# First modulation of an adaLN block cut in two by feature, its gate row spread by 32-row groups

## What is computed

```python
x = L0_attn_data                                   # (2, 512, 512) f32
mod = (_silu(L0_c) @ L0_wmod).reshape(2, 6, 1, -1)  # c (2, 512), wmod (512, 3072)
sa, ca, ga, sb, cb, gb = (mod[:, 0], mod[:, 1], mod[:, 2], mod[:, 3], mod[:, 4], mod[:, 5])
ga = (2 * (ga >= 0) - 1) * jnp.maximum(jnp.abs(ga), 0.25)     # gb likewise
h = _layernorm(x) * (1 + ca) + sa
x = x + ga * (h @ (weight * block_mask).T + bias)   # 512x512, mask in 32x32 blocks
h = _layernorm(x) * (1 + cb) + sb
x = x + gb * ffn(h)      # silu(h w1') * (h w3') w2', each w with a rank-16 addition, HID 1376
```

## Time and profile before

| what | value |
|---|---|
| time, median of 3 runs | 253.67 us (253.4 to 253.71) |
| the profiled execution's own time | 253.31 us |
| its span, first to last instruction | 251.5 us |
| PE busy | 244.5 us (97%) |
| DVE, ACT, POOL busy | 134.3, 90.0, 96.8 us |
| granted TensorE clock | 0.996 of full |
| packets moved | 24.02 MB, mean 96 GB/s |

### The profile page before, as it was taken

The page is one execution under the profiler, slowest core; times in us unless marked ns, Lnnn a source line. Parts: engine busy times, 40 slices in busy tenths (PEclk is TensorE's granted clock), DMA queues, the critical chain, the costliest instruction groups (busy, mean ns, idle before and its releaser), DMA issues.

```text
span 251.5 us, 3398 instructions
## 1 busy us (share of the span) xinstructions
PE 244.5 (97%) x1202; PEld 193.4 (77%) x1202; DVE 134.3 (53%) x215; ACT 90.0 (36%) x152; POOL 96.8 (38%) x102
## 2 busy tenths in 40 slices
PE   7999999998999999999999999999999999999993
PEld 6757876886888888888888778888888888888772
DVE  3568599899899854654654631741233123312224
ACT  2358563843423465465432412122212221222110
POOL 1329792326423130330310360497356335633300
PEclk9999999999999999999999999999999999999998
DMA  6999990022324413313317630040000000000005
GB/s 187 385 367 408 414 384 21 3 86 83 83 83 126 128 42 122 85 46 116 92 46 106 44 19 0 12 154 0 3 1 0 0 0 3 0 0 0 3 1 168
DMA packets 12529, 24.02 MB, mean 96 GB/s; under 512 B 1240, under 2 KB 2648, under 8 KB 12512
## 3 DMA queue, kind: packets, MB, share of 16 engines
q1 hardware_dynamic: 12352, 23.65, 30.2%
q10 hardware_dynamic: 160, 0.15, 0.3%
HBM read 21.18 MB, written 2.10 MB: 93 GB/s over the span
## 4 chain that ended last, share of the span: by engine, by line
PE 88%; DMA 4%; DVE 2%; POOL 1%; SPq 1%; issue 1%; ACT 1%; DVEq 0%; POOLq 0%; ACTq 0%
PE up_b L1114 24%; PE up_a L1114 24%; PE acc L1128 8%; PE acc L1129 8%; PE acc L1127 8%; DMA wa<-in_weight 4%; PE acc L1064 4%; PE side L1095 2%; POOL ht_lo L399 1%; DVE xt L806 1%; PE side L1099 1%; PE side L1064 1%; PE acc L967 1%; PE up_a L991 1%; PE acc L1027 1%
## 5 line engine op out<-in xcount | busy, mean ns | idle before, releaser
L904 DVE TENSOR_TENSOR g<-up_b,g 128x512 f32<-128x512 f32 (+1 forms) x22 | 15.2, 690 | 64.5 <-PE up_b L1114 64.5
L1128 PE MATMUL acc<-w_lo,g_hi 128*128 128x512 f32 (+1 forms) x88 | 34.7, 394 | 0.0
L1129 PE MATMUL acc<-w_hi,g_lo 128*128 128x512 f32 (+1 forms) x88 | 34.7, 394 | 0.0
L1127 PE MATMUL acc<-w_hi,g_hi 128*128 128x512 f32 (+1 forms) x88 | 34.6, 394 | 0.0
L654 ACT ACTIVATE g<-up_a 128x512 f32<-128x512 f32 (+1 forms) x22 | 13.1, 597 | 58.8 <-PE up_a L1114 58.8
L794 DVE SCALAR_TENSOR_TENSOR raw<-side,raw 128x512 f32<-128x512 f32 (+2 forms) x33 | 21.5, 677 | 22.9 <-PE side L1095 16.3
L661 ACT ACTIVATE g_hi<-g 128x512 fp32r<-128x512 f32 (+1 forms) x22 | 13.9, 633 | 49.1 <-DVE g L904 49.1
L442 POOL TENSOR_TENSOR w_lo<-work,w_hi 128x512 fp32r<-128x512 f32 (+1 forms) x11 | 14.2, 1287 | 41.3 <-ACT w_hi L580 41.3
L573 ACT ACTIVATE w_hi<-raw 128x512 fp32r<-128x512 f32 (+2 forms) x33 | 20.3, 627 | 21.7 <-DVE raw L794 21.6
L908 DVE TENSOR_TENSOR g_lo<-g,g_hi 128x512 fp32r<-128x512 f32 (+1 forms) x22 | 22.7, 1033 | 8.7 <-ACT g_hi L661 8.4
L1114 PE MATMUL up_a<-ht_hi,w_lo 128*128 128x512 f32 (+1 forms) x88 | 24.2, 396 | 1.1 <-DVE w_lo L800 1.1
(11 more groups left out here) (161 smaller groups left out, 381.5 us busy)
## 6 DMA issues: line engine op xcount, KB each, us to landing
raw<-in_ffn SPq DMA_DIRECT2D x33, 256.0 KB, 2.7
wmod_sb<-in_wmod SPq DMA_DIRECT2D x4, 1024.0 KB, 11.5
xt<-in_x SPq DMA_DIRECT2D x8, 256.0 KB, 8.2
wmod_sb<-in_wmod SPq DMA_DIRECT2D x1, 2048.0 KB, 15.7
out<-xt SPq DMA_DIRECT2D x8, 256.0 KB, 2.5
mask_sb<-in_mask SPq DMA_DIRECT2D x4, 256.0 KB, 9.8
wa<-in_weight SPq DMA_DIRECT2D x4, 256.0 KB, 9.9
lora_raw<-in_lora SPq DMA_DIRECT2D x1, 512.0 KB, 10.4
```

Of the source, the lines that this page charges most:

```text
L904: nc.vector.tensor_tensor(g[0:w], up_b[0:w], g[0:w], ALU.mult).then_inc(g_ready, 1)
L1127: nc.tensor.matmul(acc[t][:], hi, down_hi[j][0:w], start=(j == 0), stop=False)
L1128: nc.tensor.matmul(acc[t][:], hi, down_lo[j][0:w], start=False, stop=False)
L1129: last = nc.tensor.matmul(acc[t][:], lo, down_hi[j][0:w], start=False, stop=(j == HT - 1))
```

## The change

SP: mask 0 is loaded ahead of the first modulation's weights. These weights are laid out anew on the host so that one 1 MB load holds shift and scale of features 0 to 255 (all rows of `wmod`), and a second, now behind masks and weights 0 and 1, those of features 256 to 511. The place of the second batch's `x`, ahead of the gate's weights, is the same in both kernels.

TensorE: each half of the first modulation has 16 matmuls of 128 columns, its own bank, copy, turn (one transpose) and `shift`/`one_plus`. Half 0 stands before the first `attend`; half 1 and the turn of chunk 3 behind `attend(0, 0, 0)`. Warm-up matmuls go from 26 to 28, fillers from five to two. The mask's block sums move, `gate_rows(0)` stands behind `attend(0, 2, 2)` instead of ahead of it, and the gate is spread by eight matmuls with 32-row operands, of which four (one for each group of rows) write four banks. The second modulation has 32 matmuls of 128 columns in place of 16 of 256.

ACT and DVE: `bias_high` and `bias_part` come first; ACT makes one more normed tile of pass 1 (DVE one less); the gate is copied by four instructions of 2 x 128 columns, one a bank; low-rank piece 1 comes later on both. POOL: the root of tiles 4 and 5 stands one step earlier, that of 6 and 7 behind the last `wa_lo`.

```diff
-WARM_MATMULS = 26
+WARM_MATMULS = 28
-GATE_COPIES = B
+GATE_COPIES = T
+CENTRED = {0: 2, 1: 2, 4: 4, 5: 4, 6: 6, 8: 8, 9: 8, 10: 10}
+NORMS_ACT = (2, 5, 8)
+NORMS_DVE = (2, 3, 4)
-FILL_TURN, FILL_H = 3, 2
+FILL_H = 2
...
+        def mods_done(q):
+            i, k = divmod(q, KT)
+            return 3 if PASSES[i][1] else 1 + k // 2
...
             load_x(0)
-            load_mod(SHIFT_A, GATE_A, wmod_a_loaded[0], slice(0, KT // 2))
             sp.dma_start(mask_sb[:, 0], mask[:, 0]).then_inc(mask_loaded[0], 16)
-            load_mod(SHIFT_A, GATE_A, wmod_a_loaded[1], slice(KT // 2, KT))
+            load_first_mod(0)
             sp.dma_start(wa[:, 0], weight[:, 0]).then_inc(wa_loaded[0], 16)
-            for k in range(1, KT):
-                load_attention(k)
+            load_attention(1)
+            load_first_mod(1)
+            load_attention(2)
+            load_attention(3)
             load_x(1)
...
             masked_weight_low(2)
             low(2)
+            root(T, 2)
             masked_weight_low(3)
-            root(T, 2)
             root(T + 2, 2)
             low(3)
...
+            def gate_copy(q):
+
+                act.wait_ge(spread_out, 1)
                 act.wait_ge(block_on_ready, KT)
-                nc.scalar.activation(gate_row_a[b], acc[2 + b][:], ACT.Copy).then_inc(gate_row_ready, 1)
+                src = acc[q][:, 2 * P:(2 + B) * P].rearrange("p (b n) -> p b n", b=B)
+                nc.scalar.activation(mask_sb[:, 0:B, q * P:(q + 1) * P].bitcast(F32), src, ACT.Copy
+                                     ).then_inc(gate_row_ready, 1)
...
             high(3)
             whole(3)
-            gate_size(0)
             norm(T)
             norm(T + 1)
-            for n in range(LORA_FIRST):
-                lora_high(n)
-            gate_copy(0)
-            gate_copy(1)
+            gate_size(0)
+            norm(T + 2)
+            lora_high(0)
+            for q in TURN_BANKS:
+                gate_copy(q)
             high(4)
...
             mask_on(2)
+            first_columns(1)
+            mask_weight(2)
             mask_sum(3)
-            mask_weight(2)
             mask_on(3)
             mask_weight(3)
             moment(4)
             moment(5)
             moment(6)
+            centres(T)
             moment(7)
-            centres(T)
             gates_of(0)
-            norm(T + 2)
+            centres(T + 2)
             norm(T + 3)
-            for n in range(LORA_FIRST):
-                lora_part(n)
+            lora_part(0)
...
+            def gate_spread():
 
                 pe.wait_ge(gates_ready, 1)
-                pe.wait_ge(h_ready, 3 + b)
-                for q in range(KT):
-                    row = q * QUAD + b
-                    last = nc.tensor.matmul(acc[2 + b][:, q * P:(q + 1) * P], ident[:, row:row + 1].broadcast_to([P, P]),
-                                            gates_a[:], start=True, stop=True)
+                pe.wait_ge(cols_ready, 2)
+                pe.wait_ge(h_ready, KT)
+                for b in range(B):
+                    for q in range(KT):
+                        rows = slice(q * QUAD, (q + 1) * QUAD)
+                        row = q * QUAD + b
+                        last = nc.tensor.matmul(acc[q][:, (2 + b) * P:(3 + b) * P],
+                                                ident[rows, row:row + 1].broadcast_to([QUAD, P]), gates_a[rows],
+                                                start=True, stop=True)
...
             pe.wait_ge(silu_c_ready, 1)
-            mod_rows_part(0, (0, 1))
+            mask_blocks(0)
+            mod_products(0, 0)
             turn(0)
+            first_columns(0)
             turn(1)
-            mask_blocks(0)
             turn(2)
-            turn(3)
-            mod_rows_part(0, (2, 3))
-            fill(FILL_TURN)
+            fill(FILL_H)
             mask_blocks(1)
-            columns(0)
-            fill(FILL_H)
             pe.wait_ge(ones_ready, 1)
             pe.wait_ge(bias_ready, 1)
             pe.wait_ge(cols_ready, 1)
             pe.wait_ge(block_on_ready, 2)
             attend_bias(0)
             attend(0, 0, 0)
+            turn(3)
+            attend(0, 0, 1)
+            mod_products(0, 1)
+            attend(0, 0, 2)
+            first_columns(1)
             mask_blocks(2)
-            attend(0, 0, 1)
-            attend(0, 0, 2)
-            mask_blocks(3)
             attend(0, 1, 0)
             attend(0, 1, 1)
+            mask_blocks(3)
             attend(0, 1, 2)
             attend(0, 2, 0)
             attend(0, 2, 1)
+            attend(0, 2, 2)
             gate_rows(0)
-            attend(0, 2, 2)
             attend(0, 3, 0)
-            gate_spread(0)
-            gate_spread(1)
+            gate_spread()
             turn(4)
```

More of the change, by code:

```diff
@@ L185, in build @@
         wa_loaded = [sem(f"wa_loaded{k}") for k in range(KT)]
-        wmod_a_loaded = [sem(f"wmod_a_loaded{h}") for h in range(2)]
+        wmod_a_loaded = [sem(f"wmod_a_loaded{f}") for f in range(2)]
         wmod_ga_loaded = sem("wmod_ga_loaded")
@@ L287, in mask_bank, with mod_out_at, cols_at @@
             return acc[0] if k >= 2 else side[0]
-        def mod_bank(second):
-            return up_a if second else up_b
+        def mod_out_at(second, f):
+            if second:
+                return up_a[:, f * P:(f + 1) * P]
+            return acc[0][:, 2 * P:3 * P] if f else up_b[:, 0:P]
+        def cols_at(second, f):
+            if second:
+                return up_a[:, HALF + f * P:HALF + (f + 1) * P]
+            return acc[0][:, 3 * P:4 * P] if f else up_a[:, 0:P]
+        def mods_done(q):
+            i, k = divmod(q, KT)
+            return 3 if PASSES[i][1] else 1 + k // 2
         def merge_bank(r):
@@ L539, in high @@
                     act.wait_ge(attn_out, T * (b + 1))
-                act.wait_ge(cols_ready, 1 + second)
+                act.wait_ge(cols_ready, mods_done(q))
                 bias_col, scale = columns_of(q)
@@ L602, in masked_weight_high @@
                 nc.scalar.activation(wa_hi[k][:], wa[:, k], ACT.Copy).then_inc(wa_high_ready, 1)
+            bias_high()
             norm(0)
             norm(1)
[L606 to L607 removed]
+            first_mod_evacuate(0)
             masked_weight_high(0)
@@ L630, in _ @@
             high(7)
-            for n in range(LORA_FIRST, len(LORA_CUTS)):
+            for n in range(1, len(LORA_CUTS)):
                 lora_high(n)
-            mod_evacuate(1)
+            mod_evacuate()
             norm(2 * T)
@@ L716, in whole @@
                 dve.wait_ge(high_ready, q + 1)
-                dve.wait_ge(cols_ready, 1 + second)
+                dve.wait_ge(cols_ready, mods_done(q))
                 if q not in (2 * KT - 2, 2 * KT - 1):
@@ L864, in _ @@
             centres(2 * T)
-            columns(1)
+            columns()
+            lora_part(1)
             centres(2 * T + 2)
@@ L979, in fill, with mod_products, first_columns, columns @@
                     nc.tensor.matmul(side[1][:], ht_lo[1][:, 0, 0:P], ht_lo[1][:, 0], start=True, stop=True)
[L981 to L988, removed]
+            def mod_products(second, f):
+                if second:
+                    pe.wait_ge(wmod_f_loaded, 16)
+                    pe.wait_ge(attn_gated, 1)
+                else:
+                    pe.wait_ge(wmod_a_loaded[f], 16)
+                    if f:
+                        pe.wait_ge(*h_done(0))
+                dst = mod_out_at(second, f)
+                for k in range(KT):
                     for q in range(4):
-                        at = ((SHIFT_A, SCALE_A), (SHIFT_F, SCALE_F))[second][q // 2] * D + q % 2 * HALF
-                        last = nc.tensor.matmul(mod_bank(second)[q * QUAD:(q + 1) * QUAD, 0:HALF], silu_c[:, k],
-                                                wmod_sb[:, k, at:at + HALF], start=(k == 0), stop=(k == KT - 1))
-                if KT - 1 in ks:
+                        at = (SHIFT_F * D if second else 0) + f * D + q * P
+                        last = nc.tensor.matmul(dst[q * QUAD:(q + 1) * QUAD], silu_c[:, k],
+                                                wmod_sb[:, k, at:at + P], start=(k == 0), stop=(k == KT - 1))
+                if f or not second:
                     last.then_inc(mod_out, 1)
-            def columns(second):
-                pe.wait_ge(mod_rows_ready, 1 + second)
-                for c in range(2):
-                    at = second * HALF + c * P
-                    last = nc.tensor.transpose(up_a[:, at:at + P], mod_rows[:, second, c * P:(c + 1) * P], ident)
+            def first_columns(f):
+                pe.wait_ge(mod_rows_ready, 1 + f)
+                nc.tensor.transpose(cols_at(0, f), mod_rows[:, 0, f * P:(f + 1) * P], ident).then_inc(cols_out, 1)
+            def columns():
+                pe.wait_ge(mod_rows_ready, 3)
+                for f in range(2):
```

(10 more changed lines are left out.)

65 lines of the change are left out of this document (36 added, 29 removed).

## The result

The changed kernel takes 257.26 us (median of 4, 256.82 to 257.71), the kernel before 253.69: ratio 1.0142, 95% interval 1.0121 to 1.0162. It is slower by 3.6 us. I had forecast 253.2 with 254.1 as the upper end, so sign and size are both wrong.

A forecast was written before the change was run, and what follows sets the result against it. PE is busy 244.5 of 251.5 us, but DVE sets the pace from 32 to 62 us; `whole(4)` 0.35 us sooner gives 252.95 from the profiled 253.31, 253.3 from the median; taken as 253.2, range 252.1 to 254.1.

The forecast's parts named there:

- Loads, warm-up and first attend: Start of the kernel: half 0 lands at 10.8 us, 1.7 us of work moves behind, first attend at 15.4 to 15.5.
- The middle chain: From `mask_blocks(2)` at 20.3 us over `high(2)` at 22.3 and POOL's root until 26.25 to `centre` at 26.45.
- `centre` 26.45. ACT: two norms ... DVE's two gate steps: Norms until 27.95 us, DVE's gate steps until 28.85, third norm until 29.75, `high(4)` at 31.3, `whole(4)` at 32.1.
- Low-rank piece 1 hidden in the wait for the root: On DVE behind `whole(4)`: some 0.65 us of work stands in the 1.15 us that DVE waits for a root.
- The spread: Gate's spread on PE: 32-row matmuls side by side take 0.55 us in place of 1.95; the 1.4 saved are idle.
- The rival that put a slower result on a serial spread: Spread doesn't run side by side, takes 1.95 us; `whole(4)` 0.4 later than before, 253.9 us; chance 0.08.
- My sign for it: The rival of a serial spread decides as soon as the spread takes over 1.2 us.
- The late stall of about 1 us stays: PE's wait for `w_lo` near 60.4 us is still about 1 us long.
- the kernel's end moves by what `whole(4)` moves: DVE sets the pace between 32 and 62 us, so the end follows `whole(4)`, not what PE saves.
- the 0.35 that I had forecast for all of it: `whole(4)` on DVE moves from 32.47 to 32.1 us, 0.35 us sooner, and the kernel's end with it.

The follow-up runs named there:

- run with 128-row operands: The version with one-input forms, low-rank pieces early and four fillers, its spread's eight matmuls given 128-row operands again: 254.45 us, ratio 1.0029.
- the run with twelve fillers: The changed kernel with 12 filler matmuls on a free bank in PE's gap ahead of the spread: 256.07 us, ratio 1.0093.
- the repaired kernel: The changed kernel with one-input centre and gate forms, and low-rank pieces 0 and 1 put early on ACT and DVE: 253.25 us, ratio 1.0002.
- both waits: The changed kernel with POOL waiting for pass 1's first centres before its last wa_lo and for the gate before low(3): 256.2 us, ratio 1.0085.
- one wait ahead of wa_lo: The changed kernel with POOL waiting for the first centres of pass 1 before its last wa_lo: 255.88 us, ratio 1.0079.
- one wait ahead of low(3): The changed kernel with POOL waiting for the gate before low(3): 255.75 us over 10 executions, ratio 1.0083.
- both pairs of centres: The changed kernel with POOL waiting for the first centres before wa_lo(3) and the second centres before low(3): 254.99 us, ratio 1.0044.
- one SBUF input: The changed kernel with the centre as two one-column tensor_scalars and the gate's sign written to PSUM, order and waits untouched: 254.09 us, ratio 1.0028.
- piece 0 later: The changed kernel with one-input centre and gate, and low-rank piece 0 moved later on ACT, DVE and POOL: 254.25 us, ratio 1.0025.
- before, new spread: The kernel before with only the gate spread by eight 32-row matmuls into four banks and copied by four instructions: 253.42 us, ratio 0.9999.
- pieces early, four fillers: The changed kernel with one-input forms, low-rank pieces 0 and 1 early, and four filler matmuls ahead of the spread: 253.09 us, ratio 0.9985.

## Why the prediction was wrong

- *Loads, warm-up and first attend.* Right to 0.5 us: 15.01 against 15.4 to 15.5. The moved 1.7 us of work stood where I put it.
- *The middle chain.* `high(2)` came at 21.48, not 22.3, and the gate's rows at 25.82, not 26.4. PE and ACT were 0.6 to 0.8 us better than forecast. The centre gained nothing by it: it started at 26.46, where I had 26.45. My chain had the root behind POOL's `low(2)` alone, but POOL then waited 0.64 us for DVE's moments, a term that I had left out. DVE was late by one more standstill, 1.19 us for `mask_weight(3)` in place of 0.69:

```profile
22.30 1.19 DVE L784 TENSOR_TENSOR wa<-wa,block_on 128x512 f32<-128x512 f32 x1
```

```profile
21.65 1.29 POOL L467 TENSOR_TENSOR wa_lo<-wa,wa_hi 128x512 fp32r<-128x512 f32 x1 [2.86 <-ACT wa_hi L628]
...
25.27 0.22 POOL L403 TENSOR_SCALAR rstd<-moments 128x2 f32<-128x2 f32 x1 [0.64 <-DVE moments L712]
```

- *"`centre` 26.45. ACT: two norms ... DVE's two gate steps".* **This step failed.** I priced the centre at 0.15 and the multiply at 0.3 us. In the rows of before, POOL was idle beside the centre and made only a root of two columns beside the multiply. The change moved both to a time at which POOL subtracts 512 columns, and they took 1.16 and 1.37 us. These two terms, sized wrong by 1.0 and 1.1 us, are most of why PE's gap was 3.07 us and not 0.5; the rest is that PE came to it 0.3 us sooner than forecast and the other gate steps ended 0.2 later. The trace of before had the evidence. Its `mask_weight(1)` took 1.13 us beside a subtraction, where the earlier trace rows have 0.69:

```profile
16.38 1.13 DVE L748 TENSOR_TENSOR wa<-wa,block_on 128x512 f32<-128x512 f32 x1
```

```profile
15.68 1.28 POOL L447 TENSOR_TENSOR wa_lo<-wa,wa_hi 128x512 fp32r<-128x512 f32 x1 [5.54 <-ACT wa_hi L602]
```

And its pair of norms from 28.95 took 1.94 us, with one of them 1.49 us long beside `low(3)`, where a norm otherwise takes 0.54.
- *The clock.* My sum held PE at 2.4 GHz. No case of mine had the gap cost more than its length; it cost 1.2 us more.
- *Low-rank piece 1 hidden in the wait for the root.* Wrong in kind: I set its cost at nothing as long as the wait outlasted it. The wait did outlast it by 1.04 us, but the piece held up the root that the wait was for. In the changed kernel the root's first step took 0.78 and not 0.23 us; with the standstills repaired, taking the piece out shortened the stretch behind `whole(4)` from 29.70 to 29.36 us.
- *The spread.* Side by side, as forecast, at 0.72 us and not 0.55; the saving alone buys nothing in the kernel before, as I had it. The rival that put a slower result on a serial spread named the wrong mechanism, though its price of 0.75 us was of the right kind: run with 128-row operands, it cost 1.1 to 1.36 us. My sign for it, a spread of over 1.2 us, was a bad one: the changed kernel's took 1.24 us while running side by side, at half the clock.
- *The late stall of about 1 us stays.* Right, 1.08 us. But "the kernel's end moves by what `whole(4)` moves" holds only in part: `whole(4)` moved by 2.41 us (32.47 to 34.88), the end by 3.9, because the slow turns also held PE back from its work for batch 1: from `whole(4)` to the end of the stall it took 30.77 us, but 29.82 in the run with twelve fillers, which kept the clock.

The ledger after the event, in medians: 1.2 us for the clock (257.26 to 256.07), 2.1 for the standstills (to 253.97), 0.8 for the place of the low-rank pieces (to 253.21, of which 0.34 behind `whole(4)`). These differences are taken across chips, whose kernels before differ by up to 0.24 us. What is left of the change lies 0.3 below the kernel before on the same chip (253.49) where the clock holds. That this is near the 0.35 that I had forecast for all of it is in part luck: the repaired kernel is another than the one I forecast, and its gaps on both sides of the spread are 1.12 and 0.73 us, where I had 0.5 and 1. What stays open: why gaps of the same kind cost the clock in one execution and not in the next. No run was made for that.

## What to carry to other kernels

A duration read from a trace belongs to what ran beside it: before a DVE operation with two SBUF inputs is moved, look whether POOL works on whole tiles at its new time, and before a POOL operation is moved, at DVE. Where such an operation must lie there, give one input from PSUM or as a pointer scalar; that was worth 2.1 us here. A wait on POOL did the same only once every meeting had one; a single wait moved the meeting to the next operation. And a gap in PE is not priced by its length alone: four fillers in a gap of 1.1 us left none of the executions that ran 1.3 to 1.8 us longer, in eleven.

## What the runs showed of the hardware

- A centre of two columns took 0.16 us alone and 1.14 to 1.20 us beside a POOL subtraction of 1.29 us, and ended with it; a multiply of 128 columns 0.29 alone and 1.37 to 1.39 beside. With one input from PSUM, or the second as a pointer scalar, 0.29 and 0.33 (for two) beside POOL. The multiply with two SBUF inputs beside POOL's root step of two columns (0.71 us) took 0.29, in five kernels.
- The 32-row matmuls on full 32-bit operands do run side by side: eight in 0.72 us at full clock, against 1.95 to 2.05 us with 128 rows, 2.7 to 2.8 times as fast, not four. Their 16 records, of 0.27 us each in the run with twelve fillers, lie over one another.
- The granted clock fell to half behind 3.07 us of idle PE and stayed there from 31 to 37 us, though PE was busy for 5.29 of these 6 us. The executions that lost it for a time (mean clock 0.993 or less) are counted below. The gaps are those of each kernel's profiled execution, so a row tells of the kernel, not of each execution. Between the two gaps PE only spreads the gate.

| kernel | gap ahead of the spread, behind it (us) | lost the clock |
|---|---|---|
| changed | 3.07, 0.59 | 4 of 4 |
| both waits | 1.02, 2.25 | 3 of 4 |
| one wait ahead of wa_lo | 1.00, 2.19 | 3 of 4 |
| one wait ahead of low(3) | 2.03, 0.58 | 6 of 10 |
| both pairs of centres | 1.03, 1.22 | 4 of 5 |
| one SBUF input | 1.11, 1.14 | 3 of 10 |
| piece 0 later | 1.13, 0.73 | 4 of 10 |
| pieces early | 1.12, 0.73 | 3 of 12 |
| before, new spread | none, 1.13 | 0 of 10 |
| pieces early, four fillers | 0.21, 0.72 | 0 of 11 |
